# The loop over pairs of blocks written out on all engines, in a state-space and mixture-of-experts layer

## The reference, cut to what matters

```python
x = L0_attn_input_states                    # 16 blocks x 256 tokens x 256
xn = layernorm(x)
# state-space branch, E = 512 channels, N = 16 states
hidden, gate = split(einsum('blh,he->bel', xn, W_in))
hidden = silu(causal_conv4(hidden) + conv_bias)
dt, Bm, Cm = split(hidden @ W_x)            # 128, 16, 16
dts = softplus(dt @ W_dt + b_dt)
state_t = exp(dts * A) * state_{t-1} + dts * Bm * hidden   # scan over 256 tokens, for each n
y = (sum_n state * Cm + hidden * D) * silu(gate)
attn = y @ W_out
# mixture of experts, all 32 experts computed, the 8 best weighted
ffn = sum_e w_e * ((silu(xn @ w_gate[e]) * (xn @ w_up[e])) @ w_down[e])
return x + attn + ffn
```

## Time and profile before

| | |
|---|---|
| time, median of 3 runs | 1488.14 us (1485.0 to 1488.45) |
| the profiled execution's own time | 1487.38 us |
| its span, first to last instruction | 1485.6 us |
| mean granted TensorE clock | 0.98 |
| instructions recorded | 29999 |
| packets of all DMA queues | 184577, 171.21 MB |

### The profile page before, as it was taken

The page is one execution under the profiler, slowest core; times in us unless marked ns, Lnnn a source line. Parts: engine busy times, 40 slices in busy tenths (PEclk is TensorE's granted clock), DMA queues, the critical chain, the costliest instruction groups (busy, mean ns, idle before and its releaser), DMA issues.

```text
span 1485.6 us, 29999 instructions
## 1 busy us (share of the span) xinstructions
PE 1360.0 (92%) x9314; PEld 1246.4 (84%) x9314; DVE 1243.0 (84%) x1580; ACT 1214.3 (82%) x2087; POOL 1274.1 (86%) x657
## 2 busy tenths in 40 slices
PE   2599999989999899998999989998999989999998
PEld 2488998979899798987989889897898979889887
DVE  3398988988989798887988978898888977889896
ACT  3788888788887788887888877888888778887874
POOL 3689899888988889898898989989799887989996
PEclk8699999999999999999999999999999999999999
DMA  5733443433434343443433434443343433434342
GB/s 131 179 98 115 118 130 104 124 105 111 124 111 122 100 115 118 114 121 102 121 111 111 123 101 120 121 122 103 105 129 104 124 103 109 121 105 121 120 122 71
DMA packets 184577, 171.21 MB, mean 115 GB/s; under 512 B 42672, under 2 KB 167632, under 8 KB 184400
## 3 DMA queue, kind: packets, MB, share of 16 engines
q1 hardware_dynamic: 150608, 121.86, 28.3%
q10 hardware_dynamic: 33792, 47.20, 11.5%
HBM read 163.72 MB, written 5.24 MB: 114 GB/s over the span
## 4 chain that ended last, share of the span: by engine, by line
PE 48%; issue 16%; ACT 15%; POOL 13%; DVE 5%; ACTq 2%; DMA 1%; SPq 0%; DVEq 0%; POOLq 0%
PE pair_ps L868 21%; PE out_ps L987 11%; PE front_ps L868 7%; POOL state L472 7%; PE turn_ps L949 5%; ACT L562 4%; ACT decay L562 4%; PE out_ps L997 4%; POOL state L481 3%; POOL moe L487 2%; ACT L570 2%; DVE u L786 2%; ACT L628 1%; ACT moe L570 1%; ACTq L545 1%
## 5 line engine op out<-in xcount | busy, mean ns | idle before, releaser
L769 DVE TENSOR_TENSOR_SCAN state<-decay,state 128x512 f32<-128x512 f32 x512 | 613.2, 1213 | 111.8 <-ACT decay L562 88.6
L472 POOL TENSOR_TENSOR state<-du,b_rep 128x1024 f32<-128x1024 f32 x256 | 610.6, 2388 | 86.8 <-DVE u L786 86.6
L562 ACT ACTIVATE decay<-dt,neg_a 128x255 f32<-128x255 f32 x1024 | 440.1, 467 | 65.2 <-DVE state L769 57.1
L987 PE MATMUL out_ps<-w_down,moe 128*128 128x256 f32 x1536 | 359.5, 380 | 0.5 <-POOL moe L487 0.5
L987 PEld LDWEIGHTS out_ps<-w_down,moe 128*128 128x128 f32 x1536 | 282.8, 190 | 34.8 <-issue 0.7
L487 POOL TENSOR_TENSOR moe<-moe,rw_rep 128x512 f32<-128x512 f32 x192 | 261.7, 1363 | 49.1 <-DVE moe L793 32.3
L949 PE MATMUL turn_ps<-ident,state 128*128 128x128 f32 x1280 | 175.7, 278 | 72.4 <-DVE state L769 38.0
L868 PE MATMUL pair_ps<-xnT_hi,w_up_hi 128*128 128x256 f32 x768 | 231.3, 301 | 7.7 <-ACT moe L570 4.9
L868 PE MATMUL pair_ps<-xnT_hi,w_gate_hi 128*128 128x256 f32 x768 | 235.9, 307 | 1.2 <-DVE moe L793 1.1
L481 POOL TENSOR_TENSOR state<-state,c_rep 128x1024 f32<-128x1024 f32 x96 | 228.1, 2376 | 9.8 <-DVE state L769 8.5
L949 PEld LDWEIGHTS turn_ps<-ident,state 128*128 128x128 f32 x1280 | 144.5, 142 | 102.3 <-issue 54.1
(11 more groups left out here) (100 smaller groups left out, 2214.6 us busy)
## 6 DMA issues: line engine op xcount, KB each, us to landing
w_down<-in_L_ffn_w_down_dram SPq DMA_DIRECT2D x384, 128.0 KB, 2.5
b_rep<-b_dram ACTq DMA_DIRECT2D x128, 256.0 KB, 3.3
rw_rep<-rw_dram SPq DMA_DIRECT2D x256, 96.0 KB, 2.5
rw_rep<-rw_dram SPq DMA_DIRECT2D x256, 64.0 KB, 2.7
c_rep<-b_dram ACTq DMA_DIRECT2D x96, 128.0 KB, 3.0
rw_rep<-rw_dram SPq DMA_DIRECT2D x256, 32.0 KB, 2.4
x_in<-L_attn_input_states_dram SPq DMA_DIRECT2D x16, 256.0 KB, 3.8
res<-L_attn_input_states_dram SPq DMA_DIRECT2D x16, 256.0 KB, 3.8
```

Of the source, the lines that this page charges most:

```text
L472: pool.tensor_tensor(state[:, n % STATES, :, :], du2[:, q, :, :], b_rep[:, n // BCH % 2, n % BCH, :][:, None, :].broadcast_to([P, ET, T]), ...
L562: last = act.activation(decay[:, h, j, 1:T], dt[:, q, e, 1:T], ACT.Exp, scale=neg_a[:, e, n:n + 1])
L769: dve.tensor_tensor_scan(x, decay[:, h, :, :].rearrange("p e t -> p (e t)"), x, 0.0, ALU.mult, ALU.add).then_inc(scanned, 1)
L987: last = pe.matmul(out_ps[:, c, :], moe[:, p % RING, j, c * P:(c + 1) * P], w_down[:, p % RING, j, :], start=(p == 0 and j == 0 and c == 0 ...
```

## The change

The hardware loops are replaced by loops of the program that writes the kernel. Each engine's stream then holds all 16 blocks one behind another; `i` is a number everywhere, so that each wait is on a constant, the second wait of `wait_alone` is gone, and there is neither a register for the round nor a branch. The order of work on each engine, the buffers, the transfers and the counts that are waited for stay as they are.

```diff
@@ blocks, for TensorE, VectorE, ScalarE and GpSimd
-            main(0, 0, True, False)
-            with eng.Fori(0, (BLOCKS - 2) // 2) as g:
-                main(2 * g + 1, 1, False, False)
-                main(2 * g + 2, 0, False, False)
-            main(BLOCKS - 1, 1, False, True)
+            for i in range(BLOCKS):
+                main(i, i % 2, i == 0, i == BLOCKS - 1)
             for a in range(SLOTS, 2 * SLOTS):
                 slot(BLOCKS - 1, 1, a)
@@ SyncE
-            main(0, 0, True, False, True)
-            with sp.Fori(0, (BLOCKS - 2) // 2 - 1) as g:
-                main(2 * g + 1, 1, False, False, True)
-                main(2 * g + 2, 0, False, False, True)
-            main(BLOCKS - 3, 1, False, False, True)
-            main(BLOCKS - 2, 0, False, False, False)
-            main(BLOCKS - 1, 1, False, True, False)
+            for i in range(BLOCKS):
+                main(i, i % 2, i == 0, i == BLOCKS - 1, i + 2 < BLOCKS)
```

## The result

The written-out kernel takes 1441.13 us (median; 1440.27 to 1443.5) against 1486.57 us of the kernel before in the same comparison: the ratio is 0.9699, with a 95% interval of 0.9676 to 0.9722. That is 45.4 us less.

A forecast was written before the change was run, and what follows sets the result against it. TensorE, busy 92% of the span, was taken to set the pace, with stalls at six back edges. 1487.38 - 24.9 (edges) - 1.1 (constants) = 1461.4 us, given as 1461.5; range 1451 to 1470 us.

The forecast's parts named there:

- The back edges: At the loop's six turns from round end to start: removing them saves 24.9 us, 4.15 each, read from the pace.
- The first window: Between the first two output projections: no back edge before its end, yet 87.10 us, so short windows aren't catching up.
- waits with constants: In the loop's fourteen blocks: waits on constants instead of registers save 14 x 0.08 = 1.1 us.
- the 0.08 us from the first unit after a turn to the third: Through ScalarE and VectorE after a turn: 8.23 us with registers, 8.15 in block 15, taken as having constants.
- the range's lower bound: 1451 us for the whole kernel; the constants' bound of 11.9 us over 14 blocks gave 1450.6 us.
- the other comparison: Same pair of units in blocks 0 and 2: 51.46 us with constants, 51.19 with registers, so 0.27 us longer.
- (a): Rival, all blocks of the loop: constants shorten every block, 11.9 us at its bound, 1450.6 us; chance 0.13.
- (b): Rival, all blocks of the loop: constants lengthen blocks as engines slow each other, 6.4 us, 1468.9 us; chance 0.10.
- (c): Rival, at the back edges: another wait stands behind the branch and comes back; time stays at 1487 us; chance 0.03.
- (d): Rival, GpSimd in each block: it fetches code it kept and stalls 3.3 us, up to 1508.7 us; chance 0.02.
- TensorE's 3.5 us of idle time a block: In a block without an edge, 87.16 - 83.68 us: the limit on further gain from waits with constants.

The follow-up runs named there:

- The first experiment: The loop kernel of before with only ScalarE's silu waits swapped, buffer first and TensorE's unit second, table load ahead of the unit's wait: 1475.77 us against 1487.56, ratio 0.9913.

## Why the prediction was wrong

**The back edges** were right in their place and their size: 24.9 us, read from the pace, and now gone, with the alternation, the issue rows of TensorE and the fallen clock (TensorE's busy time in the twelve windows is 6.9 us lower for the same matmuls). The first window did show the pace of a kernel without edges, as far as edges go. What the working had not seen is that the parts are no terms of a sum. It gave 2.34 us to TensorE, 1.09 to ScalarE and 0.3 to the rest; taken away alone, TensorE's gave 0.9 us an edge and VectorE's nothing. The total was right because it was taken from the pace.

**The step that failed** is the one on waits with constants, and in it the sentence on the 0.08 us from the first unit after a turn to the third. It took block 15's 8.15 us for a turn with constants. But the silu that holds this stretch stands in slot -1 of its block, so block 15's is issued in the last slot of block 14, inside the loop, with a register. The stretch compared a register with a register, and the range's lower bound (11.9 us at most, 1450.6 us) rested on it. The pair of turns that does compare them was in the trace: into block 1, whose silu is issued by the written-out block 0, the table load is done before the unit (149.43 to 150.7, shown above), into every later block it isn't. By the same distance between units the pair differs by 1.2 us (7.0 for 8.2), where the prediction had 0.08 us. Slot -1 also explains why the other comparison, between 93.08 and 144.54 us, showed no gain: pair 0's silu lies outside it. Its 0.27 us to the other side has not come back in the written-out kernel, where only block 0 is as slow.

So the term for the waits stood in the sum at 14 x 0.08 = 1.1 us, as arithmetic and nothing else. As arithmetic it is worth 2 to 3 us over the run (0.15 to 0.19 us a block). What the change did beside it was to swap the two waits around a table load, worth 17.4 us, by an order of waits that the source text doesn't show.

**The rivals.** (a) had the right sign and the wrong mechanism and bound: the blocks got shorter by 1.4 us, not by 0.85 at most, and at one place, not everywhere. (b) didn't happen. (c) is refuted by the run with two rounds: one edge for six, the same waits in twelve of the fourteen blocks (the other two were put at 2.7 us), 20 us less. (d) is refuted: with GpSimd written out the windows are all alike and no stall is seen, and its loop in place of the straight code made the kernel some 2.8 us slower, not faster. TensorE's 3.5 us of idle time a block, given as the limit of any gain beside the edges, held.

**What stays open.** The first experiment's 7 us are accounted for by the edges' windows. That single edges of the kernel before take 3.3 to 6.0 us goes with the clock: the three windows at 1.00 are 90.50 to 90.95 us, the two at 0.98 are 91.30 and 91.92, and the one at 0.96 is 93.19. Why it fell over some edges and not over others is open, and so is the branch of 6.0 us. The run with two rounds is 4 us above its expectation. Two windows hold this: the one over its edge is 93.16 us (clock 0.96), 6 us above the straight ones instead of 4.15, and the window of its tail is 2.4 us longer than before (72.06 us for 69.66); the run with all but ScalarE written out has a longer one too (72.1 us), and no run shows why.

## What to carry to other kernels

Read the price of a loop's back edge from the pace of equal blocks with and without one, and don't add up the stalls of the engines: they lie side by side, and the next longest takes the place of the one removed. Where two waits stand in front of an activation that changes its table, see to it that the wait that ends last is on the activation, and the table load ahead of it: one swapped pair of waits was worth as much as four back edges. And before two stretches are compared as with and without a feature, find out for the instruction that holds each of them where it is issued; in an order with slots below zero that is another block.

## What the runs showed of the hardware

A taken branch of TensorE's sequencer lasted 4.3 us (median; 6.0 us in the run with two rounds and the earlier table load). That of VectorE and ScalarE is recorded with 63 and 50 ns, and what follows shows only as the gap to the sequencer's next instruction: 3.3 us on VectorE, and 2.9 us on ScalarE (327.5 to 330.4 us), of which up to 2.4 us lay on the chain. That the gap is a fetch of code is a reading; the extra packets of the instruction queues over the edge agree with it. Behind the branches of GpSimd and SyncE (45 ns) the next instruction of the loop came within 0.3 us.

The Trainium skill, "Advanced Engine Details and Errata", section "Control Flow Timing", has 108 ns for a compare-and-branch. The 45 to 63 ns recorded on four engines lie below it, and what a taken branch cost TensorE, VectorE and ScalarE lies far above.

Between the first output projection and the last full block, TensorE's granted clock fell to its lower level (1.2 GHz) in the windows that hold an edge and in no other: in three of six before, in all six with TensorE's stream alone written out, and nowhere in the written-out kernel. In a window at 0.98 the same matmuls are busy some 1.5 us longer, in one at 0.96 some 3.2 us.

A table load took 1283 ns in all 128 cases of L562 and ran without waiting for what its activation waits for, if no wait was put ahead of it.
